# A two-layer graph network on one core: the first weights' loads, tile 0's products and the edge counts put in another order

## The reference

```python
h = lnw * (x * rsqrt(mean(x * x) + 1e-6))        # T5 norm, weight lnw
out = h @ W_root + bias                           # 1024 x 286
for r in range(2):
    w = (edge_type_2 == r)
    sums = segment_sum((h[src] @ W_rel[r]) * w, dst)
    out += sums / max(segment_sum(w, dst), 1)
x = layernorm(x + x + elu(out) @ wo)
# second layer: the same with 8 relations of edge_type_8, weights 1024 x 1024,
# then u, a gate z = concat(u, x) @ w_gate, h = tanh(u) * z + x * (1 - z)
x = layernorm(x + h)
```

## Time and profile before

| | us |
|---|---|
| median of 3 runs | 864.94 (864.93 to 864.95) |
| the profiled execution | 865.18 |
| its span | 863.4 |
| PE busy | 823.8 (95%) |
| DVE busy | 678.1 (79%) |
| ACT busy | 437.6 (51%) |
| mean granted TensorE clock | 0.989 |

### The profile page before, as it was taken

How to read it: one execution, slowest core, us unless ns; L and a number is a source line. 1 busy time by engine, 2 the same in 40 slices (tenths; PEclk the granted TensorE clock), 3 DMA queues, 4 the chain that set the end, 5 groups by cost and what they waited for, 6 DMA issues and landing times.

```text
span 863.4 us, 15952 instructions
## 1 busy us (share of the span) xinstructions
PE 823.8 (95%) x6316; PEld 585.5 (68%) x6316; DVE 678.1 (79%) x977; ACT 437.6 (51%) x613; POOL 15.5 (2%) x38
## 2 busy tenths in 40 slices
PE   3699999999989999999999999999999999999996
PEld 1366664547867686786776876867868768678544
DVE  6999688699786777867768778777787787778996
ACT  3676764736653545535535455355354453554711
POOL 1000000000000000000000000000000000000000
PEclk9799999999999999999999999999999999999999
DMA  9100262122112112022022020220220202305811
GB/s 306 62 1 2 78 231 84 56 91 72 65 61 98 55 44 98 1 97 97 0 97 69 29 97 0 97 97 0 97 87 10 97 16 84 122 2 146 195 49 70
DMA packets 41067, 66.09 MB, mean 77 GB/s; under 512 B 11606, under 2 KB 15314, under 8 KB 41027
## 3 DMA queue, kind: packets, MB, share of 16 engines
q1 hardware_dynamic: 39639, 64.09, 21.8%
q10 hardware_dynamic: 1388, 1.44, 0.5%
HBM read 57.71 MB, written 5.18 MB: 73 GB/s over the span
## 4 chain that ended last, share of the span: by engine, by line
PE 75%; DVE 17%; ACT 5%; issue 2%; DMA 1%; ACTq 0%; DVEq 0%; POOL 0%; POOLq 0%
PE psP L1110 44%; PE psA L1176 20%; PE psP L943 7%; PE psA L932 2%; DVE wsplit L1351 2%; DVE p_mem L1388 1%; DMA stage<-in_L_gnn_W_rel 1%; PE psP L1035 1%; DVE wsplit L1345 1%; ACT wsplit L648 1%; DVE p_mem L1389 1%; DVE wsplit L1455 1%; DVE xT L1316 1%; DVE cu_mem L1585 1%; PE psP L903 1%
## 5 line engine op out<-in xcount | busy, mean ns | idle before, releaser
L1110 PE MATMUL psP<-wsplit,xT 128*128 128x256 f16 x2592 | 294.9, 273 | 2.6 <-DVE p_mem L1632 1.9
L1110 PEld LDWEIGHTS psP<-wsplit,xT 128*128 128x128 f16 x2592 | 253.5, 98 | 36.0 <-DVE p_mem L1632 2.2
L1176 PE MATMUL psA<-p_mem,cu_mem 128*128 128x512 f16 x800 | 177.0, 381 | 2.3 <-DVE cu_mem L1616 2.3
L1110 PE MATMUL psP<-wsplit,x 128*128 128x256 f16 x1296 | 150.3, 273 | 0.0
L1176 PEld LDWEIGHTS psA<-p_mem,cu_mem 128*128 (+1 forms) x800 | 78.6, 98 | 94.7 <-DVE cu_mem L1616 2.8
L1110 PEld LDWEIGHTS psP<-wsplit,x 128*128 128x128 f16 x1296 | 126.8, 98 | 14.7
L1351 DVE SCALAR_TENSOR_TENSOR wsplit<-stage,sc,wsplit 128x1024 f16<-128x1024 f32 x90 | 114.8, 1279 | 26.7 <-ACT wsplit L648 26.7
L648 ACT ACTIVATE wsplit<-stage,sc 128x1024 f16<-128x1024 f32 x90 | 100.6, 1137 | 16.1 <-DVE sc L1246 10.2
L1616 DVE SCALAR_TENSOR_TENSOR cu_mem<-psA,coef,cu_mem 128x512 f32<-128x512 f32 x80 | 60.0, 750 | 33.5 <-PE psA L1176 31.6
L648 ACT ACTIVATE wsplit<-x,sc 128x1024 f16<-128x1024 f32 x54 | 61.8, 1144 | 45.6 <-PE psP L1110 31.6
L1351 DVE SCALAR_TENSOR_TENSOR wsplit<-x,sc,wsplit 128x1024 f16<-128x1024 f32 x54 | 69.2, 1282 | 11.1 <-ACT wsplit L648 10.9
(11 more groups left out here) (203 smaller groups left out, 796.8 us busy)
## 6 DMA issues: line engine op xcount, KB each, us to landing
stage<-in_L_gnn_weight SPq DMA_DIRECT2D x16, 2048.0 KB, 7.8
stage<-in_L_gnn_w_gate SPq DMA_DIRECT2D x4, 2048.0 KB, 8.0
x_home<-x SPq DMA_DIRECT2D x5, 512.0 KB, 2.6
x<-x_home SPq DMA_DIRECT2D x5, 512.0 KB, 7.2
x<-in_x SPq DMA_DIRECT2D x4, 512.0 KB, 9.7
xT<-in_L_gnn_root SPq DMA_DIRECT2D x1, 2048.0 KB, 9.1
stage<-in_L_gnn_root SPq DMA_DIRECT2D x1, 2048.0 KB, 7.7
out<-x SPq DMA_DIRECT2D x4, 512.0 KB
```

The lines of the kernel that those rows point to most:

```text
L1110: last = nc.tensor.matmul(psP[:, bank, (col + tt) * FB:(col + tt + 1) * FB], lhs[tt](a, c), split_block(n, b)[:, c, :], start=(first and t ...
L1176: last = nc.tensor.matmul(psA[:, (NT * h + t) % 2, :], cnt8[:, r, s, t * P:(t + 1) * P], p_part[h][a][:, s, :], start=(s == 0 and a == 0), ...
```

## The change

The first weights are loaded in four parts of two chunks. On ACT's queue the relation parts of the first load stand ahead of the edge types; on SP's queue all edge loads still stand first. ACT sums chunks 0 and 1, squares x tile 0, sums chunks 2 and 3, and squares x tile 1 before the high halves. The norm of tile 0 stands ahead of the order checks on DVE.

Tile 0 has its own routine on PE: as each chunk is split, its left products are made, and its right products three chunks later (`LAG`). No counts stand beside it. The 32 batches stand in tiles 1 to 4, with three one-hot buffers (`OH_RING`) instead of two, the third in memory that is free by then. `first_sums(t - 1, 1)` stands behind the first batch of the next tile instead of ahead of it.

```diff
-BESIDE = ((0, 0, 2, 2), (2, 2, 2, 2), (2, 1, 2, 2), (2, 1, 2, 2), (2, 2, 2, 0))
-W0_PARTS = ((0, 4), (4, 6), (6, 8))
+BESIDE = ((0, 0, 0, 0), (2, 2, 2, 2), (2, 2, 2, 2), (2, 2, 2, 2), (2, 3, 3, 0))
+W0_PARTS = ((0, 2), (2, 4), (4, 6), (6, 8))
+LAG = 3
+OH_RING = 3
...
             load_edges(sp, ((DST, dst_d), (SRC, src_d)), nodes_loaded)
+            load_last_edges(sp, ((DST, dst_d), (SRC, src_d)), nodes_loaded)
...
             act.dma_start(lnw[:, :], lnw_d.rearrange("(c p) -> c p", p=P)).then_inc(lnw_loaded, 16)
-            load_edges(act, ((TYPE8, t8_d), (TYPE2, t2_d)), types_loaded)
             for r in range(R0):
                 w0_load(act, 0, 1 + r, wrel_d[r])
+            load_edges(act, ((TYPE8, t8_d), (TYPE2, t2_d)), types_loaded)
+            load_last_edges(act, ((TYPE8, t8_d), (TYPE2, t2_d)), types_loaded)
...
-                act.wait_ge(keys_gathered, 2)
-                for n, types, bank in ((R1, slice(0, R1), 4), (R0, slice(R1, REL_ALL), 3)):
+                for n, types, bank, gathered in ((R1, slice(0, R1), 4, 1), (R0, slice(R1, REL_ALL), 3, 2)):
+                    act.wait_ge(keys_gathered, gathered)
...
-            w0_sums_first()
+            w0_chunk_sums(0)
             square_x(0)
+            w0_chunk_sums(1)
             spread_keys()
             split_hi(0, 0, xT, X_GAIN)
+            square_x(1)
             act.wait_ge(w0_scaled, 1)
             w0_high(0)
             w0_high(1)
+            split_hi(0, 1, xT, X_GAIN)
+            q_high(0, 0)
+            q_high(0, 1)
...
-            for t in range(NT - 1):
+            for t in range(1, NT - 1):
                 copy_tile(t)
...
+            def first_tile():
+
+                pe.wait_ge(q_done, 3)
+                pe.wait_ge(turned_split, 2)
+                for c in range(DC + LAG):
+                    if c < DC:
+                        pe.wait_ge(w0_lo, c + 1)
+                        last = product(psA[:, 0, 0:FH], xT, U_W0, 0, slice(0, FH), (c,))
+                    if c == DC - 1:
+                        last.then_inc(q_full, 1)
+                    if c >= LAG:
+                        last = product(psA[:, 1, 0:FH], xT, U_W0, 0, slice(FH, F3), (c - LAG,))
+                    if c == DC // 2:
+                        pe.wait_ge(flag_ready, 1)
+                        turn(0, 1, xs, xs_ready)
+                last.then_inc(q_full, 1)
+
...
-            for t in range(NT - 1):
+            first_tile()
+            for t in range(1, NT - 1):
                 count_tile(t)
...
-            def onehot_batch(k, b):
-                dve.wait_ge(win_counted, 2 * k + 2)
+            def onehot_batch(k):
+                if k >= OH_RING:
+                    dve.wait_ge(win_counted, 2 * (k - OH_RING) + 6)
...
             spread_low()
+            norm_x(0)
             order_checks()
-            w0_sum(1)
-            norm_x(0)
             w0_sum(2)
+            w0_sum(3)
...
-            split_lo(0, 0, xT, X_GAIN)
-            dve.wait_ge(wrong_counted, 1)
-            nc.vector.tensor_reduce(flag[:, :], psC[0:1, 0:RUN + KT], AX.X, ALU.max).then_inc(flag_ready, 1)
+            split_lo(0, 0, xT, X_GAIN, (0,))
+            dve.wait_ge(w0_sums, DC // 2 + 1)
+            nc.vector.memset(acc0[:, :, F:FPAD], 0.0).then_inc(acc_padded, 1)
...
+            split_lo(0, 0, xT, X_GAIN, (1,))
+            dve.wait_ge(scale_step, 4)
+            step(ts(ci[:, 0:1], sc_f[:, U_W0, 3:4], 1.0 / X_GAIN, None, ALU.mult))
+            ts(ci[:, 1:2], ci[:, 0:1], 1.0 / PROD_GAIN, None, ALU.mult).then_inc(ci_ready, 1)
...
             w0_low(0)
+            dve.wait_ge(wrong_counted, 1)
+            nc.vector.tensor_reduce(flag[:, :], psC[0:1, 0:RUN + KT], AX.X, ALU.max).then_inc(flag_ready, 1)
+            norm_x(1)
+            dve.wait_ge(convb_loaded, 16)
+            step(ts(convb[:, :], convb[:, :], 1.0, None, ALU.add))
             w0_low(1)
...
-                if t:
-                    first_sums(t - 1, 1)
...
-                        onehot_batch(k, b)
+                        onehot_batch(k)
+                        if n == 0 and m == 0:
+                            first_sums(t - 1, 1)
...
-            for t in range(NT):
+            split_lo(0, 1, xT, X_GAIN)
+            first_sums(0, 0)
+            for t in range(1, NT):
                 onehot_tile(t)
```

More of the change, by code:

```diff
@@ L176, in build @@
         kf_at = ANY_RING * ANY * (P + BANK_COLS) // 2
-        oh_lo = p_f16(lo_at, P, 2, BATCH, P)
-        oh_key = p_f16(key_at, P, 2, BATCH, MCOLS)
+        oh_lo = [p_f16(lo_at + n * BATCH * P // 2, P, BATCH, P) for n in range(2)]
+        oh_key = [p_f16(key_at + n * BATCH * MCOLS // 2, P, BATCH, MCOLS) for n in range(2)]
         key_spread = p_f16(spread_at, P, NWIN, REL_ALL)
@@ L277, in build @@
         turned_split = sem("turned_split")
-        w0_loaded = [sem(f"w0_loaded{a}") for a in range(3)]
+        w0_loaded = [sem(f"w0_loaded{a}") for a in range(len(W0_PARTS))]
         w0_sums = sem("w0_sums")
@@ L425, in slot_load, with edge_span, load_last_edges @@
             return 16 * ((i + 1) // 2)
+        def edge_span(v, p0, p1):
+            return bass.AP(v.tensor, v.offset + p0 * RUN, [[RUN, p1 - p0], [1, SPAN]])
         def load_edges(engine, arrays, loaded):
-            def span(v, p0, p1):
-                return bass.AP(v.tensor, v.offset + p0 * RUN, [[RUN, p1 - p0], [1, SPAN]])
             for a, v in arrays:
-                engine.dma_start(edges[0:ROWS16, a, :], span(v, 0, ROWS16)).then_inc(loaded, 16)
+                engine.dma_start(edges[0:ROWS16, a, :], edge_span(v, 0, ROWS16)).then_inc(loaded, 16)
+        def load_last_edges(engine, arrays, loaded):
             engine.wait_ge(edges_padded, 2)
             for a, v in arrays:
-                engine.dma_start(edges[ROWS16:EP - 1, a, :], span(v, ROWS16, EP - 1)).then_inc(loaded, 16)
+                engine.dma_start(edges[ROWS16:EP - 1, a, :], edge_span(v, ROWS16, EP - 1)).then_inc(loaded, 16)
                 engine.dma_start(edges[EP - 1:EP, a, 0:RUN], v[EDGES - RUN:EDGES].unsqueeze(0)).then_inc(loaded, 16)
@@ L673, in _, with w0_chunk_sums @@
             st0, hi0, _ = unit_weights(U_W0)
-            def w0_sums_first():
+            def w0_chunk_sums(a):
                 act.wait_ge(lnwT_ready, 1)
-                act.wait_ge(w0_loaded[0], 48)
-                for c in range(DC // 2):
+                act.wait_ge(w0_loaded[a], 48)
+                for c in range(*W0_PARTS[a]):
                     nc.scalar.activation(w0_land[:, c, :], st0[:, c, :], ACT.Abs, scale=lnwT[:, c:c + 1],
@@ L902, in count_batch @@
                         jj = i * BANK_WINS + j
-                        last = nc.tensor.matmul(out[:, :, j * PCOLS:(j + 1) * PCOLS], oh_lo[:, b, jj, :],
-                                                oh_key[:, b, jj, :].rearrange("p (s w) -> p s w", s=NT),
+                        last = nc.tensor.matmul(out[:, :, j * PCOLS:(j + 1) * PCOLS], oh_lo[k % OH_RING][:, jj, :],
+                                                oh_key[k % OH_RING][:, jj, :].rearrange("p (s w) -> p s w", s=NT),
                                                 start=(j == 0), stop=False, skip_group_check=True)
@@ L1273, in _ @@
                    ALU.is_equal).then_inc(ident_ready, 1)
+            dve.wait_ge(lnw_turned, 1)
+            nc.vector.tensor_copy(lnwT[:, :], psC[:, 0:DC]).then_inc(lnwT_ready, 1)
             dve.wait_ge(nodes_loaded, 96)
@@ L1308, in order_checks, with split_lo @@
                 tt(wrong[:, RUN:RUN + KT], tops[:, :], dst[:, P - 1:SPAN:STEP], ALU.is_ge).then_inc(wrong_ready, 1)
-            def split_lo(k, t, dst, gain):
-                for g in range(2):
+            def split_lo(k, t, dst, gain, groups=(0, 1)):
+                for g in groups:
                     n = 2 * NT * k + 2 * t + g
@@ L1461, in _ @@
             dve.wait_ge(keys_spread, 2)
-            nc.vector.memset(acc0[:, :, F:FPAD], 0.0).then_inc(acc_padded, 1)
-            dve.wait_ge(scale_step, 4)
-            step(ts(ci[:, 0:1], sc_f[:, U_W0, 3:4], 1.0 / X_GAIN, None, ALU.mult))
-            step(ts(ci[:, 1:2], ci[:, 0:1], 1.0 / PROD_GAIN, None, ALU.mult))
-            dve.wait_ge(convb_loaded, 16)
-            step(ts(convb[:, :], convb[:, :], 1.0, None, ALU.add))
             def onehot_tile(t):
-                if t:
-                    first_sums(t - 1, 1)
                 for n in range(4):
```

14 lines of the change are left out of this document (7 added, 7 removed).

## The result

The changed kernel took 858.58 us (median of 6 runs, 857.54 to 861.02), the kernel before 864.07 (6 runs, the three of the table above and three more, 862.94 to 864.95); the ratio is 0.9945, with a 95% interval of 0.9929 to 0.9961. It is faster by 5.5 us; 7.9 was forecast. In the profiled execution (858.35 us, span 856.6) the four terms came out as follows. The times are those of the timelines; the degrees, 101.16 in the chain of waits, begin at 101.00 there in the kernel before.

A forecast was written before the change was run, and what follows sets the result against it. Only the first 101 us matter, bound by DVE and PE taking turns until PE leaves the counting stage. −4.3 + 1.7 − 5.4 + 0 = −8.0 us from 865.18 gave 857.2, as median 857.0; range 854.5 to 861.0.

The forecast's parts named there:

- Term A: Preparation: the first weights' scale is ready earlier, at 21.4 instead of 25.73; −4.3 us, bounds −4.7 and −2.7.
- Term B: Split of the first weights, from scale ready to the last low half: longer by 1.7 us, from 9.35 to 11.05.
- Term C: From the last low half to the last one-hot: less DVE work and waiting, −5.4 us, bounds −7.4 and −3.5.
- R1: Rival: DVE's wait moves to ACT's split, 0.8 in each of tiles 1 to 4 or so; 858.9 us, chance 0.14.
- Term D: Behind the last one-hot, one batch of counts and twelve products, 2.86 us: no change, 0.
- R4: Rival: PE's clock stays at half through tile 0 into tile 1; slower, some 868 us, chance 0.04.
- T: The time at which `w0_scale` is ready, 25.73 before the change and forecast at 21.4.
- T + 7: Sign of a wrong forecast: the clock still at half beyond 7 us after `w0_scale` is ready.
- R5: Rival: more gain, edge types landing by 8.6 and no waits; 854.7 us, chance 0.05.

The follow-up runs named there:

- v2_reduce_first: The changed kernel with GpSimd's first all-reduce (`spare`) put ahead of its six iotas; ratio to the kernel before 0.9942.
- v1_square_early: The changed kernel with `square_x` of tiles 2 to 4 moved on ACT to just behind the previous tile's first `split_hi`; ratio to the kernel before 0.9918.
- v4_all_three: The changed kernel with early squares, GpSimd's all-reduce first and ACT's wo sum moved from tile 4 to tile 3; ratio to the kernel before 0.9922.
- v3_pe_kept_busy: The changed kernel with 44 products that nothing reads added on PE ahead of tile 0's; ratio to the kernel before 0.9937.
- w3_square_and_reduce: The changed kernel with the early squares and GpSimd's all-reduce first; ratio to the kernel before 0.9922.

## Why the prediction was right, and where it was off

The sign, the place and the range were right, and the four terms of the sum have the signs forecast. The sum was 8.0 us, the traced stage gave 5.2. Two terms carry the difference.

**Term A** (−4.3, measured −3.2). DVE's chain was right to 0.1 us at its end, but that is luck, of two misses that cancel: the types came before they were asked for (KEY8 without a wait at 9.55, where 9.9 was forecast), and the sources 1.0 us late, which the text had not counted. The step that failed is "the two small products 0.4, half of `split_lo(0,0)` 0.65, the memset 0.47, and 0.98 from the reduce of `ar`", in which POOL's maximum is taken to hide under DVE's work. It does before, where it starts at 23.49. With the sums at 19.4 it stands behind POOL's first all-reduce at 20.63 and DVE waits 0.97. That this wait is the cause is shown by v2_reduce_first, in which it goes and the scale comes at 21.43, 1.07 earlier, which is the 21.4 of the forecast. Its size differs between executions, as `spare` starts anywhere from 19.6 to 21.3: from the end of DVE's sums to the scale are 2.0 us with GpSimd's order changed, 3.1 in the changed kernel, and 2.0 to 3.6 in the others with its GpSimd order and its small first load.

**Term B** (+1.7, measured +1.4) was right in mechanism. The `convb` step took 0.30 instead of 0.41, and the gaps were smaller.

**Term C** (−5.4, measured −3.9). The work was right (55.5 for 55.8). The waits were put at 1.95 us and were 3.5: 1.0 for 0.65 and 0.4 for 0.4 at tile 0, but 1.9 at the norm and 0.2 at the split where the text had "I take 0.3 in each of three tiles", 0.9, at the split. The step that failed is "what is late next is ACT: `split_hi` stands behind four bank copies". ACT is late next, but sooner in the list: `square_x(t + 1)` stands behind the copies of the last two batches, and DVE, which the sums no longer hold at the start of the tile, asks for the norm before it is ready. R1 named the right shape, a wait that takes the place of the one removed, and nearly its size (0.8 for 0.93), but put it at the wrong instruction and in four tiles instead of two. v1_square_early shows the place: with the square moved 1.15 us are gained, and only then is the rest at the split.

**Term D** (0, measured +0.5). "Tile 4: ACT's 3.0 us sum over wo delays copies, but DVE is three batches ahead; 0." DVE was, PE was not: three batches a part need banks sooner, and the last counts waited for a copy. The chain of waits shows it; v4_all_three takes it away there and shows that it then costs more in tile 3, 0.8 us for 0.5.

**The tile 0 order** and **the three buffers** do what the forecast says: undone, they cost 1.1 and 1.3 us, the place of the sums 1.8, the loads 5.0. These do not add up to 5.2: the ring and the place of the sums remove the same wait, and `norm_x(0)` ahead of the sums is a loss without the small first load. The two DVE changes together give 1.3 us in the kernel before; what either gives there alone was not run. Of the 2.0 us in the changed kernel that leaves, by subtraction, 0.7 for tile 0 and the moved batches. Undoing tile 0's order alone costs 1.1, so these parts overlap too; the moved batches by themselves were not run.

**The clock (R4)**: it fell at about 21.7, 4.3 us after PE went idle (2.4 in the kernel before), and rose at about 28.5, T + 6.0, where the forecast had it; v3_pe_kept_busy shows that the half clock in tile 0 costs nothing. The second profile of the changed kernel says so too. There it rose only at about 30.6, T + 7.7, past the T + 7 that the prediction had as a sign of being wrong, and the degrees came 73.3 us after the scale all the same. The Trainium skill (TensorE: Matmul & The Clock Gate, What's actually happening) says that the moment of the change differs from run to run. The trace agrees, with 28.5 and 30.6 for the rise in one and the same kernel, and it shows more: behind the same 2.3 us of idleness at the first aggregation one profile of the changed kernel has the half clock and the other has not.

Three readings of the prediction are off, without weight for the sum. The rise of the clock in the kernel before, put at 31.7, is at 31.5 in the earlier trace rows (0.75 over the stretch from 31 to 32), after 3.4 us of products and not 3.7. A loss of 1.7 us would give 866.6 and not R4's 868. And R5's terms (−4.7, +1.7, −7.4) make 854.5, the range's lower end, and not 854.7.

What stays open is why the edges' landing moved between 5.9 and 7.0 us in kernels with this load order, what sets the start of `spare` between 19.6 and 21.3, and whether all times of the changed kernel above 860 us have the half clock at 252 us, since only one of them was profiled.

## What to carry to other kernels

When a wait in an in-order list is removed, walk down the list of the engine that is now early and ask of each next wait when its releaser was ready in the old trace: here the square root was ready just in time, and the slack of 0.8 us that hid it was the very wait removed. Look also at units that seemed idle in the old trace: POOL's maximum had 2.3 us to spare and became the bound when its input came 3.9 us sooner. And compare marks inside a profile, here the time from the scale to the degrees, which repeated to 0.1 us between executions, when the times themselves scatter by more than the effect.

## What the runs showed of the hardware

GpSimd stands still for long before some first instructions, with no instruction shown for it. In the 11 profiles with GpSimd's old order these gaps are 7.2 to 9.7 us before the first iota (behind memsets) and 7.35 to 9.1 before the first all-reduce behind the iotas; with the all-reduce first they are 7.25 to 7.4 before the first iota (v2_reduce_first, v4_all_three, w3_square_and_reduce). There is none before an all-reduce that stands behind memsets only (1.96 in these three). In the same three the next all-reduce behind the iotas starts 6.0 to 6.1 us after its input is there, at about 91 us (77 in v4_all_three), where it is 0.2 in the changed kernel. The Trainium skill (GPSIMD Engine Reference, Instruction dispatch) says that the first call of newly loaded code costs about 6 us that no instruction in the profile shows. The trace agrees with the 6.0 to 6.1, and has more, 7.2 to 9.7, in the first 30 us. That these gaps are the loading of code is not shown by any run here.

The granted clock can fall to 1.2 GHz behind a wait of 2.3 us or stay at 2.4: it fell in nine of the 14 profiles, where 30 products then took 8.2 to 8.3 us, and stayed in five, where they took 6.65.

Twelve loads of 286 KB kept up: ACT's second pair of sums began at 11.72, where about 12 was forecast, and both of DVE's reduces ran from 15.18 without a wait for their data.
